# A plan of expert blocks worked out one stage earlier, and fewer clearings of semaphores between stages

## Chip, cores and metric

One core of one Trainium2 chip. The metric is the device time of one execution in microseconds. Its median over three runs of the kernel before is 2325.03 us.

## What is computed

Two layers, each an attention part and a mixture-of-experts part, over 16 sequences of 512 tokens and 128 features. After each part the result is added to its input and normalised:

```python
x = layernorm(x + L0_attn(x))   # cumulative sums over the sequence, 16 heads
x = layernorm(x + L0_ffn(x))    # top-1 of 8 experts, relu MLP 128-256-128
x = layernorm(x + L1_attn(x))   # softmax attention, 16 heads, position bias
x = layernorm(x + L1_ffn(x))    # shared swiglu + top-1 of 8 swiglu experts
```

In the expert parts every token goes through the one expert that its router picks: `expert = argmax(logits)`, `out[t] = MLP_expert[t](x[t])` (times a probability in the first layer, on an input times a score in the second).

## The kernel before

The program runs five stages one after the other (`program`, lines 2171 to 2219): `attention_one`, `experts` with tag b, `attention_two`, `experts` with tag d, and `finish`. Each stage has its own block of per-engine programs (`with nc.Block()`, lines 284, 938, 1249, 2042), at whose end every engine drains and all meet at a barrier. Behind it the helper `stage` (lines 2186 to 2191) lets GpSimd clear the stage's semaphores (line 2189) and then holds a second barrier of all engines (line 2190), five times in all, the last time behind `finish`.

Both attention stages loop over the 16 sequences and route their tokens at the end of each: VectorE keeps a running count of each expert's tokens (`keep.run`), works out the slot of every token, and GpSimd scatters the rows by indirect DMA to `xs_d` or `zs_d` (lines 647 and 1367, four DMAs for each sequence), so that every expert has a region of its own. At the end of the stage GpSimd waits for its scatters.

`experts` works in 24 blocks of 512 rows. Which expert and which rows a block has follows from the counts, so VectorE first works out a **plan** (lines 977 to 1015): some 20 small operations on 128x8, 128x24 and 128x192 elements, with a wait for its own semaphore between most of them. They make the two integer tables `expert` and `row` (24 entries each), and `offs`. GpSimd sets a tile of ones for it (line 967). SyncE waits for `plan_ready` 1 (the table `expert`) and 2 (the table `row`), and then, for each block, reads one value of each table into registers (line 906) and starts the load of the block's rows `x` (line 953) and of the expert's weights `w` (line 954), up to four blocks ahead of the work; the output goes out at line 959. TensorE turns the rows (line 1093), multiplies by the first weights (line 1085) and the second (line 1106), ScalarE and VectorE evict. After the plan VectorE also computes `keep.rows` (lines 1021 to 1034), which the next stage's gathers read. In the first expert stage GpSimd meanwhile splits and spreads a line of position biases for `attention_two` (lines 910 to 936), with loads and stores on its own queue.

What sets the order at a boundary, in SyncE's program of `experts`:

```python
sp.wait_ge(sem("plan_ready"), 1)
...
e = which(sp, expert, s.b, E - 1)
if isinstance(s.b, int) and s.b == 0:
    sp.wait_ge(sem("plan_ready"), 2)
r = which(sp, row, s.b, SPARE)
...
sp.dma_start(x[s.par][:], rows_of(src, r)).then_inc(sem(f"x_in{s.par}"), 16)
```

Of the kernel before, what the change touches and what calls it, by code (L numbers as in the profile page):

```python
# [14 lines left out]
I32 = mybir.dt.int32  # L15
# [4 lines left out]
P = 128  # L20
# [29 lines left out]
class Step:  # L50
# [3 lines left out]
    def __init__(self, b, half, par, mod=2):  # L54
        self.b, self.half, self.par, self.mod = b, half, par, mod
# [112 lines left out]
    own.wait()  # L168


def clear_rows(eng, name, b, io, done):

    regions = io[name][0:SPARE, :].rearrange("(e r) w -> e r w", e=E)
    eng.dma_start(regions[:, bass.ds(GROUP * b, GROUP), :].rearrange("e (p t) w -> p e (t w)", t=T),
                  io["zeros"].unsqueeze(1).to_broadcast([P, E, T * W])).then_inc(done, 16)
# [6 lines left out]
def attention_one(nc, g, keep):  # L182
# [9 lines left out]
    with ExitStack() as ctx:  # L192
        def sb(name, shape, dt=F32):
            return ctx.enter_context(nc.sbuf_tensor(name, shape, dt))
# [10 lines left out]
        total_ps = misc[:, T * E:2 * T * E].rearrange("p (t e) -> p t e", t=T)  # L205
        sel_ps = misc[:, 2 * T * E:3 * T * E].rearrange("p (t e) -> p t e", t=T)

        wk = sb("wk", [P, 3 * H])
        wv = sb("wv", [P, HA])
        wo = sb("wo", [P, HA // P, W])  # L210
# [73 lines left out]
        with nc.Block() as block:  # L284
# [396 lines left out]
            def _(dve):  # L681
# [158 lines left out]
                own.wait()  # L840
                own.did(v.tensor_copy(keep.run[:], runs[:, 0, :]))
                own.wait()


def experts(nc, g, keep, tag, src, dst, weights, gated):
# [14 lines left out]
    def sem(name):  # L860
        return g.sem(f"{tag}_{name}")

    with ExitStack() as ctx:
        def sb(name, shape, dt=F32):
            return ctx.enter_context(nc.sbuf_tensor(f"{tag}_{name}", shape, dt))
# [4 lines left out]
        count = sb("count", [P, E])  # L870
        blocks = sb("blocks", [P, E])
        ones8 = sb("ones8", [P, E])
        ends = sb("ends", [P, E])
        offs = sb("offs", [P, E])
        first = sb("first", [P, E])
        past = sb("past", [P, BLOCKS, E])
        ef = sb("ef", [P, BLOCKS])
        isf = sb("isf", [P, BLOCKS, E])
        rowf = sb("rowf", [P, BLOCKS])
        spare = sb("spare", [P, BLOCKS])  # L880
        row = sb("row", [P, BLOCKS], I32)
        expert = sb("expert", [P, BLOCKS], I32)
# [22 lines left out]
        def which(eng, table, n, top):  # L905
            return eng.value_load(table[0:1, bass.ds(n, 1)], min_val=0, max_val=top)
# [31 lines left out]
        with nc.Block() as block:  # L938

            @block.sync  # L940
            def _(sp):
                sp.wait_ge(sem("plan_ready"), 1)

                def step(s, on):
                    if on[0]:
                        e = which(sp, expert, s.b, E - 1)
                        if isinstance(s.b, int) and s.b == 0:
                            sp.wait_ge(sem("plan_ready"), 2)
                        r = which(sp, row, s.b, SPARE)
# [12 lines left out]
                for k in range(4):  # L962
                    sp.wait_ge(sem(f"y_out{k}"), 16 * BLOCKS // 4)

            @block.gpsimd
            def _(pool):
                nc.gpsimd.memset(ones8[:], 1.0).then_inc(sem("ones8_ready"), 1)
                if not gated:
                    split_line(pool)
                    spread_line(pool)  # L970

            @block.vector
            def _(dve):
                v = nc.vector
                own = Own(dve, sem("own"), sem("dve_passed"))
                dve.wait_ge(sem("ones8_ready"), 1)
                own.did(v.tensor_scalar(offs[:], keep.iota[:], float(REGION), None, ALU.mult))
                own.did(v.tensor_scalar(first[:], keep.iota[:], float(REGION), None, ALU.mult))
                own.wait()

                own.did(v.tensor_tensor(count[:], keep.run[:], offs[:], ALU.subtract))
                own.wait()
                own.did(v.tensor_scalar(blocks[:], count[:], GROUP - 1.0, 1.0 / GROUP, ALU.add, ALU.mult))
                own.wait()
                own.did(v.tensor_scalar(blocks[:], blocks[:], 0.5 / GROUP - 0.5, None, ALU.add))
                own.wait()
                own.did(v.tensor_scalar(blocks[:], blocks[:], ROUND, ROUND, ALU.add, ALU.subtract))
                own.wait()
                own.did(v.tensor_tensor_scan(ends[:], ones8[:], blocks[:], 0.0, ALU.mult, ALU.add))
                own.wait()  # L990

                many = [P, BLOCKS, E]
                own.did(v.tensor_tensor(past[:], keep.turn[:].unsqueeze(2).to_broadcast(many),
                                        ends[:].unsqueeze(1).to_broadcast(many), ALU.is_ge))
                own.wait()
                own.did(v.tensor_reduce(ef[:], past[:], AX, ALU.add))
                own.did(v.tensor_tensor(count[:], ends[:], blocks[:], ALU.subtract))
                own.wait()
                v.tensor_scalar(expert[:], ef[:], E - 1.0, None, ALU.min).then_inc(sem("plan_ready"), 1)

                own.did(v.tensor_tensor(isf[:], keep.iota[:].unsqueeze(1).to_broadcast(many),
                                        ef[:].unsqueeze(2).to_broadcast(many), ALU.is_equal))
                own.did(v.scalar_tensor_tensor(offs[:], count[:], -float(GROUP), offs[:], ALU.mult, ALU.add))
                own.did(v.tensor_scalar(spare[:], ef[:], E - 0.5, None, ALU.is_ge))
                own.did(v.tensor_scalar(rowf[:], keep.turn[:], float(GROUP), None, ALU.mult))
                own.wait()
                own.did(v.tensor_scalar(spare[:], spare[:], float(SPARE), None, ALU.mult))
                own.did(v.tensor_tensor(past[:], offs[:].unsqueeze(1).to_broadcast(many),
                                        rowf[:].unsqueeze(2).to_broadcast(many), ALU.add))
                own.wait()  # L1010
                own.did(v.tensor_tensor(past[:], past[:], isf[:], ALU.mult))
                own.wait()
                own.did(v.tensor_reduce(rowf[:], past[:], AX, ALU.add))
                own.wait()
                v.tensor_tensor(row[:], rowf[:], spare[:], ALU.add).then_inc(sem("plan_ready"), 1)
                dve.wait_ge(sem("plan_ready"), 2)


                pairs = [P, NB * T, E]
                slots = keep.slots[:].unsqueeze(2).to_broadcast(pairs)  # L1020
# [9 lines left out]
                own.did(v.tensor_tensor(its[:], its[:], offs[:].unsqueeze(1).to_broadcast(pairs), ALU.mult))  # L1030
# [85 lines left out]
def attention_two(nc, g, keep):  # L1116
# [20 lines left out]
    with ExitStack() as ctx:  # L1137
        def sb(name, shape, dt=F32):
            return ctx.enter_context(nc.sbuf_tensor(f"c_{name}", shape, dt))
# [10 lines left out]

        wq, wk, wv, wout = (sb(n, [P, W]) for n in ("wq", "wkk", "wvv", "wout"))
        gw = sb("gw", [P, E])
        x1 = sb("x1", [P, T, W])
        yb = sb("yb", [P, T, W])
        rows = sb("rows", [P, T], U32)
# [93 lines left out]
        with nc.Block() as block:  # L1249
# [467 lines left out]
            def _(dve):  # L1717
# [271 lines left out]
                route_last(s)  # L1989
                route_runs(s)  # L1990
                route_slots(s)


def finish(nc, g, keep):
# [180 lines left out]
def program(nc, io, stages=5):  # L2175
    g, keep = Bag(), Bag()
    g.io = io
    with ExitStack() as ctx:
# [4 lines left out]
                sems[name] = nc.alloc_semaphore(name=name)  # L2183
            return sems[name]

        def stage(run, *args):

            run(nc, g, keep, *args)
            nc.clear_and_free_semaphores(list(sems.values()))
            nc.all_engine_barrier()  # L2190
            sems.clear()

        def sb(name, shape, dt=F32):
            return ctx.enter_context(nc.sbuf_tensor(name, shape, dt))
# [9 lines left out]
        keep.prob = sb("prob", [P, NB * T])  # L2204
        keep.slots = sb("slots", [P, NB * T])
        keep.rows = sb("rows", [P, NB * T], U32)
        keep.bias = sb("bias", [P, H, DELTA, P])
        stage(attention_one)
        keep.line = sb("spread_line", [P, H, DELTA, UPAD], BF16)
        if stages >= 2:  # L2210
            stage(experts, "b", "xs_d", "ys_d", "wb", False)
        if stages >= 3:
            stage(attention_two)
        if stages >= 4:
            stage(experts, "d", "zs_d", "us_d", "wd", True)
        if stages >= 5:
            stage(finish)


_SCRATCH = {"line_d": ([H, DELTA * UPAD], F32), "bias_d": ([H, P, DELTA, P], F32), "x1_d": ([NB, P, T, W], F32), "xs_d": ([ROWS, W], F32),  # L2220
# [79 lines left out]
```

## Time and profile before

| | us |
|---|---|
| median of three runs (2323.05 to 2331.76) | 2325.03 |
| the profiled execution, whole | 2327.71 |
| its span, first to last instruction | 2325.9 |
| TensorE busy | 1985.4 (85%) |
| VectorE busy | 1502.4 (65%) |
| ScalarE busy | 1078.8 (46%) |
| GpSimd busy | 807.6 (35%) |
| mean granted TensorE clock | 0.939 of full speed |

The stages lie one behind the other in the span: the first ends at 628, the second at 765, the third at 2037 and the fourth at 2192 us. Register, branch, semaphore and DMA-issuing instructions do not count as busy; a view of one line shows them with their durations, with a q behind the engine's name for its sequencer.

### The profile page before, as it was taken

How to read it: one execution, taken by the hardware profiler on the slowest of the kernel's cores; microseconds unless marked ns; L12 is line 12 of the kernel's file. 1: busy time of each engine (PE TensorE's matmuls, PEld its weight loads, DVE VectorE, ACT ScalarE, POOL GpSimd, SP SyncE). 2: the span in 40 equal slices, each digit the busy share in tenths (PEclk: the TensorE clock that was granted, in tenths of full speed). 3: DMA queues.
4: the chain of work that ended last, by engine and by line, in shares of the span. 5: the costliest groups of instructions: out<-in, count | busy, mean ns of one | idle time of the engine just before them, and what ended most of it. 6: DMA issues, size and time to landing. Idle time of an engine off the chain costs nothing. (4 is left out here: it accounts for less than half of the span.)

```text
span 2325.9 us, 49229 instructions
## 1 busy us (share of the span) xinstructions
PE 1985.4 (85%) x15436; PEld 1034.3 (44%) x15436; DVE 1502.4 (65%) x4596; ACT 1078.8 (46%) x2723; POOL 807.6 (35%) x827
## 2 busy tenths in 40 slices
PE   8488787877388499999999999999999999679886
PEld 6255555655356133334333333334333433356554
DVE  6268878888511577777767767677677767233276
ACT  3355565565133045555555555455555555322221
POOL 4458888888400302221222122212221120100176
PEclk9689999999699699999999999999999999889998
DMA  3453232222187222322132213322232211144332
GB/s 111 153 181 109 105 104 100 75 104 98 45 229 221 91 72 80 100 84 95 61 97 92 87 61 96 95 85 86 72 103 82 96 59 64 56 140 158 115 104 86
DMA packets 127737, 235.72 MB, mean 101 GB/s; under 512 B 17622, under 2 KB 45286, under 8 KB 126966
## 3 DMA queue, kind: packets, MB, share of 16 engines
q1 hardware_dynamic: 118440, 208.51, 27.2%
q0 software_dynamic: 9072, 24.41, 3.7%
q8 instruction: 117, 1.92, 0.3%
q14 instruction: 108, 0.88, 0.1%
HBM read 185.88 MB, written 121.95 MB: 132 GB/s over the span
## 5 line engine op out<-in xcount | busy, mean ns | idle before, releaser
L1622 ACT ACTIVATE c_pT<-c_u 128x512 f32<-128x512 f32 x1024 | 574.6, 596 | 552.1 <-PE c_u L1429 552.1
L1777 DVE CUSTOM_DVE_ANT_0 c_sums<-c_s,bias 128x512 f32<-128x512 f32 x1024 | 665.1, 687 | 254.2 <-PE c_s L1411 229.5
L1411 PE MATMUL c_s<-c_kst,c_qst 126*128 126x512 bf16 x1024 | 319.0, 389 | 16.9 <-issue 11.5
L1429 PE MATMUL c_u<-spread_line,c_pick 128*32 128x512 bf16 x4096 | 317.2, 387 | 0.0
L1443 PE MATMUL c_o<-c_pT,c_vst 128*32 128x256 f32 x4096 | 310.9, 381 | 0.6 <-ACT c_pT L1622 0.5
L1421 PE MATMUL c_u<-c_qst,c_kst 128*128 128x512 bf16 x1024 | 307.7, 381 | 0.2 <-ACT c_pT L1622 0.2
L523 ACT ACTIVATE v<-a_bank,gain 128x64 f32<-128x64 f32 x768 | 166.4, 345 | 54.9 <-DVE vp L737 54.9
L1367 POOL DMA_INDIRECT zs_d<-c_xs,c_slot x64 | 63.4, 991 | 328.0 <-DMA zs_d<-in_zeros 190.6
L1443 PEld LDWEIGHTS c_o<-c_pT,c_vst 128*32 128x32 f32 x4096 | 123.1, 110 | 107.4 <-ACT c_pT L1622 4.0
L389 PE MATMUL a_bank<-wv,xT 128*128 128x512 f32 x256 | 154.1, 690 | 19.1 <-ACT v L523 14.2
L590 POOL TENSOR_TENSOR q<-q,vp 128x1024 f32<-128x1024 f32 x48 | 125.0, 2604 | 105.6 <-DVE vp L737 104.8
L1429 PEld LDWEIGHTS c_u<-spread_line,c_pick 128*32 128x32 bf16 x4096 | 61.8, 94 | 217.7 <-issue 217.7
L1421 PEld LDWEIGHTS c_u<-c_qst,c_kst 128*128 128x128 bf16 x1024 | 100.2, 98 | 121.1 <-issue 5.8
L1411 PEld LDWEIGHTS c_s<-c_kst,c_qst 126*128 126x128 bf16 x1024 | 82.7, 100 | 158.9 <-DVE c_tops L1777 101.9
L601 POOL TENSOR_TENSOR s<-q,v 128x1024 f32<-128x1024 f32 x48 | 143.3, 2985 | 0.2
L531 ACT COPY oT<-a_bank 128x512 f32<-128x512 f32 x128 | 69.4, 587 | 150.0 <-PE a_bank L410 149.9
L737 DVE TENSOR_TENSOR vp<-a_bank,ez 128x512 f32<-128x512 f32 x96 | 64.8, 687 | 106.8 <-PE a_bank L389 105.0
L418 PEld LDWEIGHTS a_bank<-wo,oT 128*128 128x128 f32 x1024 | 126.7, 199 | 14.4 <-issue 14.4
L418 PE MATMUL a_bank<-wo,oT 128*128 128x128 f32 x1024 | 129.2, 282 | 0.0
L753 DVE TENSOR_TENSOR o<-o,r 128x1024 f32<-128x1024 f32 x64 | 124.5, 1965 | 0.0
L410 PE MATMUL a_bank<-ident,o 128*128 128x128 f32 x512 | 79.2, 305 | 52.6 <-DVE o L753 51.8
L1356 POOL TENSOR_TENSOR c_rstd<-c_ve,minus_half 128x4 f32<-128x4 f32 x16 | 16.7, 1046 | 298.4 <-DVE c_ve L1746 298.4
(266 smaller groups left out, 2901.3 us busy)
## 6 DMA issues: line engine op xcount, KB each, us to landing
xs_d<-in_zeros SPq DMA_DIRECT2D x16, 2048.0 KB
zs_d<-in_zeros SPq DMA_DIRECT2D x16, 2048.0 KB, 10.0
c_kst<-parts_d SPq DMA_DIRECT2D x192, 96.0 KB
c_qst<-parts_d SPq DMA_DIRECT2D x192, 96.0 KB
parts_d<-c_parts SPq DMA_DIRECT2D x32, 384.0 KB, 3.1
d_w<-in_wd SPq DMA_DIRECT2D x24, 384.0 KB, 3.2
b_w<-in_wb SPq DMA_DIRECT2D x24, 321.0 KB, 4.6
bias_d<-line_d SPq DMA_DIRECT2D x16, 448.0 KB
```

Of the source, the lines that this page charges most:

```text
L389: nc.tensor.matmul(v_ps[h][:], xT[s.par][:, t, :], wv[:, 512 * h:512 * h + 512], start=True, stop=True).then_inc(sem("v_ready"), 1)
L418: mm = nc.tensor.matmul(y_ps[:, t * W:(t + 1) * W], oT[t % 2][:, k, :], wo[:, k, :], start=(k == 0), stop=(k == HA // P - 1))
L523: ins = nc.scalar.activation(dst[:, h * A:(h + 1) * A], v_ps[half][:, k * A:(k + 1) * A], ACT.Copy, scale=gain[s.par][:, t, h:h + 1])
L590: nc.gpsimd.tensor_tensor(q[:, t, :], q[:, t - 1, :], vp[t % 2][:], ALU.add).then_inc(sem("q_ready"), 1)
L601: nc.gpsimd.tensor_tensor(s1[s.par][:, t, :], q[:, t - 1, :], v2[t % 2][:], ALU.add).then_inc(sem("s1_ready"), 1)
L753: v.tensor_tensor(heads(o[t % 2][:]), heads(o[t % 2][:]), r[s.par][:, t, :].unsqueeze(2).to_broadcast([P, H, A]), ALU.mult).then_inc(sem(" ...
L1411: nc.tensor.matmul(s_ps[bank_of(n)][:], qst[0:ROWS_MAX, h, t * P:(t + 1) * P], kst[0:ROWS_MAX, h, :], start=True, stop=True).then_inc(sem( ...
L1421: nc.tensor.matmul(u_ps[bank_of(n)][:], kst[:, h, c * P:(c + 1) * P], qst[:, h, :], start=True, stop=False, skip_group_check=True)
L1429: mm = nc.tensor.matmul(u_ps[bank_of(n)][ARRAY * k:ARRAY * (k + 1), :].rearrange("k (t q) -> k t q", t=T), pick[:], line[:, G * j + i, T - ...
L1443: mm = nc.tensor.matmul(o_ps[ARRAY * i:ARRAY * (i + 1), half * 2 * P:(half + 1) * 2 * P], vst[s.par][:, c, f:f + ARRAY], pT[r % 2][:, i, h ...
L1622: nc.scalar.activation(pT[n // G % 2][:, n % G, :], u_ps[bank_of(n)][:], ACT.Exp).then_inc(sem("exp_done"), 1)
L1777: v.tensor_tensor_reduce(sums[n % 2][:], s_ps[bank_of(n)][:], bias, 1.0, -3.0e38, ALU.add, ALU.max, top_s[j % 2][:, k:k + 1]).then_inc(sem ...
```

## The change

A new function `plan` holds the operations of the plan, with its own memset of the ones on VectorE. It is called at the end of VectorE's program in `attention_one` (behind the copy to `keep.run`) and in `attention_two` (behind the slots of the last sequence). The tables `expert`, `row` and `offs` are kept across stages; the scratch tiles are allocated in the attention stages. `experts` loses the operations, the memset on GpSimd and both waits of SyncE. The clearing of semaphores with its barrier is now called once between the stages, ahead of `attention_two`, and once at the end; behind `attention_one`, `attention_two` and the second `experts` only the block's own barrier is left.

```diff
+def plan(v, own, keep, p):
+    many = [P, BLOCKS, E]
+    own.did(v.memset(p.ones8[:], 1.0))
+    own.did(v.tensor_scalar(keep.offs[:], keep.iota[:], float(REGION), None, ALU.mult))
+    own.wait()
+    own.did(v.tensor_tensor(p.count[:], keep.run[:], keep.offs[:], ALU.subtract))
...
+    own.did(v.tensor_scalar(keep.expert[:], p.ef[:], E - 1.0, None, ALU.min))
...
+    own.did(v.tensor_tensor(keep.row[:], p.rowf[:], p.spare[:], ALU.add))
+    own.wait()
@@ attention_one, end of VectorE's program
                 own.did(v.tensor_copy(keep.run[:], runs[:, 0, :]))
                 own.wait()
+                plan(v, own, keep, planner)
@@ experts, SyncE
-                sp.wait_ge(sem("plan_ready"), 1)
-
                 def step(s, on):
                     if on[0]:
-                        e = which(sp, expert, s.b, E - 1)
-                        if isinstance(s.b, int) and s.b == 0:
-                            sp.wait_ge(sem("plan_ready"), 2)
-                        r = which(sp, row, s.b, SPARE)
+                        e = which(sp, keep.expert, s.b, E - 1)
+                        r = which(sp, keep.row, s.b, SPARE)
@@ experts, GpSimd
-                nc.gpsimd.memset(ones8[:], 1.0).then_inc(sem("ones8_ready"), 1)
@@ experts, VectorE
-                dve.wait_ge(sem("ones8_ready"), 1)
-                own.did(v.tensor_scalar(offs[:], keep.iota[:], float(REGION), None, ALU.mult))
                 own.did(v.tensor_scalar(first[:], keep.iota[:], float(REGION), None, ALU.mult))
                 own.wait()
-                own.did(v.tensor_tensor(count[:], keep.run[:], offs[:], ALU.subtract))
...
-                v.tensor_tensor(row[:], rowf[:], spare[:], ALU.add).then_inc(sem("plan_ready"), 1)
-                dve.wait_ge(sem("plan_ready"), 2)
@@ attention_two, end of VectorE's program
                 route_slots(s)
+                own.wait()
+                plan(v, own, keep, planner)
@@ program
-        def stage(run, *args):
-            run(nc, g, keep, *args)
+        def clear():
             nc.clear_and_free_semaphores(list(sems.values()))
             nc.all_engine_barrier()
             sems.clear()
+        def stage(run, *args):
+            run(nc, g, keep, *args)
...
         if stages >= 3:
+            clear()
             stage(attention_two)
...
         if stages >= 5:
             stage(finish)
+        clear()
```

## Rows read from the trace of the kernel before

**Rows 1.** Waits, 600 to 640 us: engine, line, waited for; us, times, longest.
```profile
PE b_bank L1093 <- DMA b_x<-xs_d: 24.3, 1, 24.3
```

**Rows 2.** Timeline, 614 to 640 us: start, us, engine, line, operation, [idle before].
```profile
615.05 0.17 DVE L841 COPY run<-runs 128x8 f32<-128x8 f32 x1
616.00 1.07 POOL L647 DMA_INDIRECT xs_d<-x,slot  x1 [3.67 <-DVE slot L800]
...
619.91 0.96 POOL L647 DMA_INDIRECT xs_d<-x,slot  x1 [0.30 <-issue]
...
628.93 0.17 DVE L977 TENSOR_SCALAR b_offs<-iota 128x8 f32<-128x8 f32 x1 [13.71 <-POOL b_ones L967]
...
633.50 0.53 DVE L1015 TENSOR_TENSOR b_row<-b_rowf,b_spare 128x24 int32<-128x24 f32 x1
...
634.82 0.36 SPq L953 DMA_DIRECT2D b_x<-xs_d  x1
...
637.72 1.11 PE L1093 MATMUL b_bank<-ident,b_x 128*128 128x128 f32 x4 [24.28 <-DMA b_x<-xs_d]
```

**Rows 3.** Line 284, first block: ns min/median/max, first and last start.
```profile
L284 POOLq DRAIN  x1: 5304/5304/5304, 622.4 to 622.4; - x1
L284 SPq EVENT_SEMAPHORE  x1: 17/17/17, 627.8 to 627.8; - x1
```

**Rows 4.** Timeline, 2028 to 2047 us.
```profile
2028.40 0.16 DVE L1878 CAST c_slot<-c_slotf 128x4 uint32<-128x4 f32 x1
...
2033.28 0.96 POOL L1367 DMA_INDIRECT zs_d<-c_xs,c_slot  x1 [0.30 <-issue]
...
2038.32 0.17 DVE L977 TENSOR_SCALAR d_offs<-iota 128x8 f32<-128x8 f32 x1 [9.75 <-POOL d_ones L967]
...
2039.62 0.36 DVE L993 TENSOR_TENSOR d_past<-turn,d_ends 128x192 f32<-128x192 f32 x1
...
2042.46 0.18 DVE L1015 TENSOR_TENSOR d_row<-d_rowf,d_spare 128x24 int32<-128x24 f32 x1
...
2043.42 0.37 SPq L953 DMA_DIRECT2D d_x<-zs_d  x1
```

**Rows 5.** Line 1249, block of attention_two.
```profile
L1249 POOLq DRAIN  x1: 1367/1367/1367, 2035.7 to 2035.7; - x1
L1249 SPq EVENT_SEMAPHORE  x1: 17/17/17, 2037.2 to 2037.2; - x1
```

**Rows 6.** Line 906, table reads of SyncE, 2037 to 2044 us.
```profile
L906 SPq TENSOR_LOAD <-d_expert x1: 480/480/480, 2040.7 to 2040.7; - x1
L906 SPq TENSOR_LOAD <-d_row x1: 274/274/274, 2042.7 to 2042.7; - x1
```

**Rows 7.** Line 2189, the clearing of semaphores, whole execution.
```profile
L2189 POOLq EVENT_SEMAPHORE_RANGE_CLEAR  x5: 156/182/418, 628.1 to 2325.0; - x5
```

**Rows 8.** Line 2189, 620 to 630 us.
```profile
L2189 POOLq EVENT_SEMAPHORE_RANGE_CLEAR  x1: 397/397/397, 628.1 to 628.1; - x1
```

**Rows 9.** Line 938, block of the second experts stage, 2190 to 2193 us.
```profile
L938 SPq EVENT_SEMAPHORE  x1: 17/17/17, 2191.6 to 2191.6; - x1
```

**Rows 10.** Line 2190, the barrier behind the clearing, 2190 to 2193 us.
```profile
L2190 SPq EVENT_SEMAPHORE  x1: 17/17/17, 2192.1 to 2192.1; - x1
```

**Rows 11.** Line 647, scatter of attention_one, all 64.
```profile
L647 POOL DMA_INDIRECT xs_d<-x,slot x64: 957/962/2815, 193.5 to 619.9; - x64
```

**Rows 12.** Timeline, 2223.6 to 2226 us, in finish.
```profile
2224.11 0.68 DVE L2161 TENSOR_TENSOR e_part<-e_x,e_routed 128x512 f32<-128x512 f32 x1
...
2224.20 1.42 POOL L2075 DMA_INDIRECT e_routed<-us_d,e_rows  x1 [0.30 <-issue]
```

**Rows 13.** Windows: stretch, length; busy us (count) per engine; clock, DMA, GB/s.
```profile
650.00:700.00 50.00, 41.27 (x227) 29.09 (x226) 6.23 (x9) 17.88 (x28) 4.43 (x9) 0.93 0.89 241
767.00:804.00 37.00, 13.77 (x27) 5.63 (x27) 19.92 (x44) 4.33 (x10) 14.54 (x18) 0.50 0.30 91
825.00:900.00 75.00, 73.83 (x732) 27.57 (x729) 52.32 (x168) 43.42 (x88) 8.99 (x11) 1.00 0.24 76
```

More of the change, by code:

```diff
@@ L168, in slots_of, with __init__ @@
     own.wait()
+class Planner:
+    def __init__(self, sb):
+        self.count, self.blocks, self.ones8, self.ends = (sb(f"plan_{n}", [P, E]) for n in ("count", "blocks", "ones8", "ends"))
+        self.past, self.isf = (sb(f"plan_{n}", [P, BLOCKS, E]) for n in ("past", "isf"))
+        self.ef, self.rowf, self.spare = (sb(f"plan_{n}", [P, BLOCKS]) for n in ("ef", "rowf", "spare"))
+def plan(v, own, keep, p):
[5 more added lines that the diff above has]
+    own.wait()
+    own.did(v.tensor_scalar(p.blocks[:], p.count[:], GROUP - 1.0, 1.0 / GROUP, ALU.add, ALU.mult))
+    own.wait()
+    own.did(v.tensor_scalar(p.blocks[:], p.blocks[:], 0.5 / GROUP - 0.5, None, ALU.add))
+    own.wait()
+    own.did(v.tensor_scalar(p.blocks[:], p.blocks[:], ROUND, ROUND, ALU.add, ALU.subtract))
+    own.wait()
+    own.did(v.tensor_tensor_scan(p.ends[:], p.ones8[:], p.blocks[:], 0.0, ALU.mult, ALU.add))
+    own.wait()
+    own.did(v.tensor_tensor(p.past[:], keep.turn[:].unsqueeze(2).to_broadcast(many),
+                            p.ends[:].unsqueeze(1).to_broadcast(many), ALU.is_ge))
+    own.wait()
+    own.did(v.tensor_reduce(p.ef[:], p.past[:], AX, ALU.add))
+    own.did(v.tensor_tensor(p.count[:], p.ends[:], p.blocks[:], ALU.subtract))
+    own.wait()
+    own.did(v.tensor_scalar(keep.expert[:], p.ef[:], E - 1.0, None, ALU.min))
+    own.did(v.tensor_tensor(p.isf[:], keep.iota[:].unsqueeze(1).to_broadcast(many),
+                            p.ef[:].unsqueeze(2).to_broadcast(many), ALU.is_equal))
+    own.did(v.scalar_tensor_tensor(keep.offs[:], p.count[:], -float(GROUP), keep.offs[:], ALU.mult, ALU.add))
+    own.did(v.tensor_scalar(p.spare[:], p.ef[:], E - 0.5, None, ALU.is_ge))
+    own.did(v.tensor_scalar(p.rowf[:], keep.turn[:], float(GROUP), None, ALU.mult))
+    own.wait()
+    own.did(v.tensor_scalar(p.spare[:], p.spare[:], float(SPARE), None, ALU.mult))
+    own.did(v.tensor_tensor(p.past[:], keep.offs[:].unsqueeze(1).to_broadcast(many),
+                            p.rowf[:].unsqueeze(2).to_broadcast(many), ALU.add))
+    own.wait()
+    own.did(v.tensor_tensor(p.past[:], p.past[:], p.isf[:], ALU.mult))
+    own.wait()
+    own.did(v.tensor_reduce(p.rowf[:], p.past[:], AX, ALU.add))
+    own.wait()
+    own.did(v.tensor_tensor(keep.row[:], p.rowf[:], p.spare[:], ALU.add))
+    own.wait()
@@ L206, in attention_one @@
         sel_ps = misc[:, 2 * T * E:3 * T * E].rearrange("p (t e) -> p t e", t=T)
+        planner = Planner(sb)
         wk = sb("wk", [P, 3 * H])
@@ L869, in experts @@
         y_ps = [b[:].rearrange("p (t w) -> p t w", t=T) for b in bank[6:8]]
[L870 to L874, printed above, removed]
-        first = sb("first", [P, E])
[L876 to L882, printed above, removed]
+        first = sb("first", [P, E])
         chosen = sb("chosen", [P, NB * T])
@@ L975, in _ @@
                 own = Own(dve, sem("own"), sem("dve_passed"))
-                dve.wait_ge(sem("ones8_ready"), 1)
-                own.did(v.tensor_scalar(offs[:], keep.iota[:], float(REGION), None, ALU.mult))
                 own.did(v.tensor_scalar(first[:], keep.iota[:], float(REGION), None, ALU.mult))
                 own.wait()
-                own.did(v.tensor_tensor(count[:], keep.run[:], offs[:], ALU.subtract))
-                own.wait()
-                own.did(v.tensor_scalar(blocks[:], count[:], GROUP - 1.0, 1.0 / GROUP, ALU.add, ALU.mult))
@@ L984, in _ @@
[L984 to L1014, printed above, removed]
-                v.tensor_tensor(row[:], rowf[:], spare[:], ALU.add).then_inc(sem("plan_ready"), 1)
-                dve.wait_ge(sem("plan_ready"), 2)
                 pairs = [P, NB * T, E]
@@ L1029, in _ @@
                 own.wait()
-                own.did(v.tensor_tensor(its[:], its[:], offs[:].unsqueeze(1).to_broadcast(pairs), ALU.mult))
+                own.did(v.tensor_tensor(its[:], its[:], keep.offs[:].unsqueeze(1).to_broadcast(pairs), ALU.mult))
                 own.wait()
@@ L1152, in attention_two @@
         gw = sb("gw", [P, E])
+        planner = Planner(sb)
         x1 = sb("x1", [P, T, W])
@@ L1991, in _ @@
                 route_slots(s)
+                own.wait()
+                plan(v, own, keep, planner)
 def finish(nc, g, keep):
@@ L2206, in program @@
         keep.rows = sb("rows", [P, NB * T], U32)
+        keep.expert = sb("expert", [P, BLOCKS], I32)
+        keep.row = sb("row", [P, BLOCKS], I32)
+        keep.offs = sb("offs", [P, E])
         keep.bias = sb("bias", [P, H, DELTA, P])
```

## The prediction

> **What bounds the kernel now.** I start with the times: the span is 2325.9 us, the profiled execution took 2327.71 with what lies around it, 2.7 above the median of 2325.03. I work out a saving against that execution and take it off both. The change touches only the boundaries between stages, so the next view is the waits around the first of them: TensorE idles 24.3 us there, and what ends the wait is the landing of the first block's rows [rows 1]. The reader should ask what that load waited for. The timeline answers [rows 2]: GpSimd issues the last scatters of attention_one from 616.0 to 620.9, VectorE, free since 615.2, does nothing until 628.93, then works on the plan until 634.03, and only then does SyncE issue the load, at 634.82; TensorE starts 2.9 us behind it. What holds the barrier until 627.8 is GpSimd's drain, 5.30 us long, at the end of its block [rows 3]. The chain at the boundary is thus: scatters, drain, block barrier, clearing, second barrier, plan, table reads, load. The third boundary has the same chain [rows 4]: VectorE free at 2028.56, last scatter issued at 2034.24, drain of 1.37 us and barrier at 2037.2 [rows 5], plan from 2038.32 to 2042.64, load at 2043.42.
>
> **The plan leaves the chain (both experts stages).** In the changed kernel VectorE runs it from 615.2 and from 2028.6, beside the scatters. It takes 5.1 us in the first place, where GpSimd's work on the bias line ran beside it, and 4.3 us in the second [rows 2, 4]. Counted with 5.1 and a small memset more (0.17, as VectorE's smallest rows), it ends at about 620.4 and 2033.8, before the barriers at 627.8 and 2037.2 [rows 3, 5]: 7.4 and 3.4 us of cover. If that cover were gone, each us of the plan would delay the barrier by one. I cost it at nothing on VectorE's side. SyncE then goes on from the block barrier. It still has to read two tables: the first read took 0.48 us, the second 0.27, and from the start of the second to the load lie 0.72 us [rows 4, 6], so 0.45 us of register work for each table and 0.48 + 0.45 + 0.72 = 1.65 us in all; I take 1.7 for the barrier's own instruction too. First load of stage b: 627.8 + 1.7 = 629.5 instead of 634.82, **5.3 us** earlier. Stage d: 2037.2 + 1.7 = 2038.9 instead of 2043.42, **4.5 us** earlier. These two differences contain the clearing and second barrier that go at those places.
>
> Does a stage that starts earlier end earlier by as much? In stage b the DMA engines are busy 0.89 of the stretch from 650 to 700 with TensorE at 41.3 of 50 us [rows 13]; both are work that follows the first load and has no fixed hour, so I shift the whole stage. GpSimd's load of the bias line stands right behind the barrier in its program (line 914), so it moves with the barrier by less than 1 us while the blocks' loads move by 5.3, and comes to lie right beside the first x load. I cost the overlap at nothing and keep up to 1 us of it for the range. VectorE's next work, `keep.rows`, also starts at the barrier and not behind the plan, so nothing on its queue gets later; GpSimd's queue loses its memset and gains nothing.
>
> **The clearing.** Behind the second experts stage the block barrier is at 2191.6 and the one behind the clearing at 2192.1 [rows 9, 10]: **0.5 us** go. The clearing itself is not constant: 0.156 to 0.418 us [rows 7], with 0.397 behind attention_one [rows 8], which has by far more semaphores in its code than the experts stages. The instruction takes longer for more semaphores, so the two clearings that stay grow: ahead of attention_two by the 0.40 of attention_one, at the end by the largest and the smallest, 0.42 + 0.16. **Back: 1.0 us.** The lower bound is nothing (one instruction whatever the range), the upper one 1.0 again if a split range needs more instructions with their drains.
>
> **What the plan does to GpSimd.** This is the cost that the trace before doesn't show directly: VectorE is now busy beside the last four scatters of each attention stage, and the barrier hangs on those. An undisturbed scatter DMA takes 0.957 us, the longest 2.815 [rows 11]; in the last stage one takes 1.42 us when a VectorE operation with both inputs in SBUF starts just ahead of it [rows 12], 0.46 longer. The Trainium skill ("SBUF — State Buffer", "Who interferes with whom") says that such a tensor_tensor shares an interface with GpSimd's reads, but infers that descriptor generation isn't stalled by it, only by two-port operations such as tensor_scalar; by it the cost would be that of the tensor_scalars, well under 1 us. The trace disagrees with the inference in the 1.42 us row. By rows: nothing is the lower bound; the upper one is all eight two-input operations of the plan, four counted with 0.18 and four with 0.36 [rows 4], 2.2 us for each boundary, 4.4 in all. I take one delay of the size of that row for each boundary, 0.46, since the plan's operations are shorter than that one: **1.0 us** for both.
>
> **The sum.** 5.3 + 4.5 + 0.5 - 1.0 - 1.0 = 8.3 us. The profiled execution would take 2319.4 us, the median 2325.03 - 8.3 = **2316.7 us**, 0.36% less. A measurement of this kernel tells about 0.5%, 11.6 us, from no change, so the likeliest outcome lies within it.
>
> **Rivals.**
>
> *A drain changes its length.* GpSimd's drain took 5.30 us behind attention_one and 1.37 behind attention_two after the same four scatters [rows 3, 5], and I can't derive either from the trace. With VectorE at work beside the scatters the lengths may change. If the long one falls to the short one, 3.9 us more go: 2312.8 us, faster by 0.53%. Chance 0.12. If the short one grows to the long one, or the scatters are held up by the full 4.4 us, 3 to 4 us less: about 2320 us. Chance 0.15. For both speaks only that the two lengths exist; against, that the scatters' own issue is the same.
>
> *The first shift is swallowed.* The DMA engines at 0.89 [rows 13] and the bias line's traffic could make the first experts stage end at nearly the same time, as its early loads only queue. Then only 4.5 + 0.5 - 2.0 us are left: 2322 us. Against: no transfer in the stage waits for a clock. Chance 0.05. That the change doesn't do what it says (SyncE still held by something after the barrier) would look the same or worse; the code has no other wait ahead of the first loads, and I give it nothing of its own.
>
> *Slower: the TensorE clock at the start of attention_two.* From 767 to 804 us the granted clock is 0.50, the lower level of 1.2 GHz, while TensorE is busy for 13.8 of 37 us; from 825 on it is 1.00, 2.4 GHz, with TensorE busy for 73.8 of 75 us [rows 13]. The stage now begins some 4 us earlier and with other phases of its loads. If the low level came back for as long a stretch, 37 us, in the dense part, half of it, 18.5 us, would be lost: 2316.7 + 18.5 = 2335 us. The point from which it decides: more than 17 us of additional low clock in the dense part undoes the saving, 40 us make it slower by over 0.5%. For it speaks that the clock does fall after sparse stretches at every boundary; against, that the work and its order inside the stage are unchanged. Chance 0.05, of which 0.03 reaches past 0.5%.
>
> **How the numbers follow.** The forecast's chance is 0.63; its own spread is 2313 to 2320 from the bounds above (4.4 or nothing for the scatters, up to 2 for the clearings, some us of the clock, which rises and falls in steps at every boundary). The range is 2310 to 2323: it takes in both drain rivals and the swallowed shift, and leaves out the clock rival and a corner on either side. Faster by over 0.5% is below 2313.4: the drain rival's 0.12 and 0.14 of the forecast's lower edge, 0.26. Slower by over 0.5%: 0.03. Within 0.5%: 0.71.
>
> **What would show it.** In the changed profile the block barrier of the first stage should stand within 1 us of 627.8, and SyncE's first load of x 1.7 us behind it, without a plan on VectorE in between; VectorE's plan should stand beside the four scatters, and those should be at 0.96 to 1.4 us each. The length of stage b and of stage d from first x load to block barrier should be within 1 us of before. The clearing ahead of attention_two should read about 0.6 us, the one at the end about 0.75. The prediction is wrong if the drains behind the attention stages are other than 5.3 and 1.4 us, if scatters wait for VectorE by more than 1 us a boundary, or if attention_two's length from its first load to its last scatter changes by more than 3 us.

## The result and the profile after

The changed kernel took 2316.68 us (median of ten runs, 2312.69 to 2323.81) against 2326.41 us for the kernel before (ten runs, 2321.38 to 2331.76): ratio 0.9964, 95% interval 0.9950 to 0.9979. That is 9.7 us less where 8.3 were forecast, a difference from no change that ten runs of each can just tell, and within the 0.5% that the text called indistinguishable.

The waits around the first boundary, from 600 to 640 us of the changed kernel (line numbers have moved; L1088 is what L1093 was):

```profile
PE b_bank L1088 <- DMA b_x<-xs_d: 19.8, 2, 18.8
POOL b_whole L954 <- POOLq L335: 7.6, 1, 7.6
```

TensorE's wait is 18.8 us instead of 24.3 [rows 1]. The timeline of the same stretch shows why:

```profile
615.31 0.16 DVE L184 TENSOR_SCALAR offs<-iota 128x8 f32<-128x8 f32 x1
...
616.03 1.07 POOL L698 DMA_INDIRECT xs_d<-x,slot  x1 [3.67 <-DVE slot L851]
...
617.40 0.96 POOL L698 DMA_INDIRECT xs_d<-x,slot  x1 [0.30 <-issue]
...
617.96 0.39 DVE L207 TENSOR_SCALAR plan_rowf<-turn 128x24 f32<-128x24 f32 x1
...
618.67 0.98 POOL L698 DMA_INDIRECT xs_d<-x,slot  x1 [0.30 <-issue]
...
619.63 0.18 DVE L217 TENSOR_TENSOR row<-plan_rowf,plan_spare 128x24 int32<-128x24 f32 x1
...
619.95 0.96 POOL L698 DMA_INDIRECT xs_d<-x,slot  x1 [0.30 <-issue]
...
629.56 0.36 SPq L989 DMA_DIRECT2D b_x<-xs_d  x1
```

The plan, 628.93 to 634.03 before [rows 2], now runs from 615.31 to 619.81 beside the four scatters, which start and end within 0.1 us of where they did. The first x load is issued at 629.56; 629.5 was forecast. The end of the first block, view of line 335:

```profile
L335 POOLq DRAIN  x1: 5304/5304/5304, 622.4 to 622.4; - x1
L335 SPq EVENT_SEMAPHORE  x1: 17/17/17, 627.9 to 627.9; - x1
```

The end of attention_two's block, line 1245:

```profile
L1245 POOLq DRAIN  x1: 1362/1362/1362, 2026.8 to 2026.8; - x1
L1245 SPq EVENT_SEMAPHORE  x1: 17/17/17, 2028.4 to 2028.4; - x1
```

SyncE's table reads behind the first barrier, line 946 from 627 to 630 us:

```profile
L946 SPq TENSOR_LOAD <-expert x1: 490/490/490, 628.0 to 628.0; - x1
L946 SPq TENSOR_LOAD <-row x1: 282/282/282, 628.8 to 628.8; - x1
```

The clearings, line 2186, whole execution:

```profile
L2186 POOLq EVENT_SEMAPHORE_RANGE_CLEAR  x2: 527/602/677, 756.2 to 2313.0; - x2
```

Both drains kept their lengths [rows 3, 5]; the table reads take 0.49 and 0.28 us, where 0.48 and 0.27 were read before [rows 6]; the two clearings that are left take 0.53 and 0.68 us, longer than any before [rows 7]. The third boundary, timeline from 2018 us:

```profile
2019.54 0.16 DVE L184 TENSOR_SCALAR offs<-iota 128x8 f32<-128x8 f32 x1
...
2023.59 0.18 DVE L217 TENSOR_TENSOR row<-c_plan_rowf,c_plan_spare 128x24 int32<-128x24 f32 x1
...
2030.02 0.37 SPq L989 DMA_DIRECT2D d_x<-zs_d  x1
```

One of the eight scatters beside the plan is longer than before, the second at this boundary, 1.08 us where it took 0.96. It starts 0.10 us into a plan operation with two inputs:

```profile
2021.71 0.35 DVE L203 TENSOR_TENSOR c_plan_isf<-iota,c_plan_ef 128x192 f32<-128x192 f32 x1
2021.81 1.08 POOL L1363 DMA_INDIRECT zs_d<-c_xs,c_slot  x1 [0.31 <-issue]
```

The span fell from 2325.9 to 2314.0 us, by 11.9. I cut both traces at the same events, SyncE's barrier instructions and first x loads; all in us:

| stretch | before | changed | less |
|---|---|---|---|
| to the block barrier of attention_one | 627.85 | 627.89 | 0.0 |
| barrier to first x load, stage b | 6.97 | 1.67 | 5.3 |
| stage b, first x load to block barrier | 130.18 | 126.39 | 3.8 |
| clearing and second barrier ahead of attention_two | 0.58 | 1.04 | -0.5 |
| attention_two | 1271.63 | 1271.38 | 0.3 |
| barrier to first x load, stage d | 6.21 | 1.65 | 4.6 |
| stage d | 148.14 | 148.10 | 0.0 |
| clearing ahead of finish | 0.55 | 0 | 0.5 |
| finish | 132.67 | 134.56 | -1.9 |
| last clearing and end | 1.11 | 1.30 | -0.2 |

The change's own places are the five boundary rows: 5.3 + 4.6 + 0.5 - 0.5 - 0.2 = 9.7 us. The 0.1 us that the longer scatter costs lies inside attention_two. The 3.8 of stage b and the 1.9 of finish are not places that the change touches, and the experiments had to say whether they belong to it.

### The profile page after: what moved, and what is told of

It is laid out like the page before. It is cut to its first block and busy times, and to the rows that moved or that the text cites. A ratio compares the mean times of both kernels' runs of the same rounds, so it can differ in the third digit from the quotient of the medians.

```text
span 2314.0 us, 49191 instructions
## 1 busy us (share of the span) xinstructions
PE 1987.7 (86%) x15436; PEld 1032.6 (45%) x15436; DVE 1502.0 (65%) x4598; ACT 1077.6 (47%) x2723; POOL 807.1 (35%) x825
```

## The experiments

**The parts alone, the change again, and a first look at the drain.** All four ran together on a chip on which the kernel before took 2374.85 us (33 runs), so they compare with one another and not with the runs above. `plan_moved_alone` clears behind every stage again:

```diff
         def stage(run, *args):
             run(nc, g, keep, *args)
+            clear()
...
         if stages >= 3:
-            clear()
             stage(attention_two)
...
-        clear()
```

> The plan is moved as in the change; semaphores are still cleared, with the second barrier, behind every stage. Theory (the gain is the plan's and its table reads' leaving the chain): the block barrier of the first stage stays at 627.9 us and the first x load comes 1.7 us behind the second barrier, at 630.4; stage d's first load 1.7 us behind its barrier too. Against before some 4.4 + 3.7 = 8.1 us less, against the full change some 1 us more: about 2318 us. Rival (the clearings carry it): within 2 us of before, about 2325 us.

Measured: 2370.46 us, ratio 0.9970 (0.9948 to 0.9992), so 4.4 us less in the median where 8 was expected, with an interval of 2 to 12 us. Its trace has the mechanism: 1.66 us from the second barrier (649.63) to the first x load (651.29), 1.64 us in stage d. By the trace the rival of the clearings falls; the total alone, with an interval that begins at 2 us, would not have settled it.

`clear_moved_alone` is the kernel before with the `clear()` of the change:

> The plan stays in the experts stages; semaphores are cleared once ahead of attention_two and once at the end. Theory: 0.9 + 0.9 + 0.5 us of clearing and barrier go, 0.4 + 0.5 us come back in the two longer clearings: 1.4 us less than before, about 2325 us, which a measurement can't tell from no change. Rival (a shorter first experts stage, 126.4 us from first load to barrier in the changed kernel against 130.2 before, comes with the clearings): 4 us or more less.

Measured: 2374.09 us, ratio 0.9988 (0.9969 to 1.0007). No difference that can be told, as expected; from block barrier to first load it has 6.07 us in stage b, 0.9 less than before. But its stage b takes 127.72 us, not 130.

`changed_again` is the changed kernel without an edit:

> The changed kernel once more, for a second trace and as the standard of this job. If the 3.8 us by which the first experts stage was shorter in its trace (126.4 against 130.2 us from first load to block barrier) belong to the change, they are there again (within 1 us); if they are chance of an execution, the stage lies anywhere between 126 and 131 us. The same for finish, 1.9 us longer than before. Total about 2317 us.

Measured: 2369.44 us, ratio 0.9973 (0.9954 to 0.9991). Stage b: 127.96 us. `changed_third` and `changed_fourth`, again the changed kernel without an edit, beside the later runs, were expected to take:

> The changed kernel, as the standard of this job and a third trace of its stages. The first experts stage has taken 126.4 and 128.0 us from first load to block barrier with it, 126.5 and 131.8 in two variants that start the same way, 130.2 and 127.7 with the plan in the stage: chance, between 126 and 132 again, and no part of the change's gain.

> The changed kernel as the standard of this job, 8 to 10 us less than before.

They took 2317.95 us (ratio 0.9955, 0.9939 to 0.9971) and 2323.33 us (0.9956, 0.9933 to 0.9978), and stage b in them 127.67 and 124.62 us. In fourteen traces, those of the runs below included, stage b lies between 124.6 and 131.8 us: with the plan inside at 130.2, 127.7 and 131.7, with the plan moved at 124.6 to 131.8. The 3.8 us of the first pair of traces are at least in part chance. The means, 129.9 us of three traces and 127.8 of eleven, would leave 2 us to the plan's place; with three traces of one kind and a spread of 7 us that stays open.

`early_drain` asks why GpSimd's drain takes 5.30 us at the end of attention_one and 1.37 at the end of attention_two, which the prediction could not derive:

```diff
                 def route_scatter(s):
+                    if isinstance(s.b, int) and s.b == NB - 1:
+                        nc.gpsimd.drain()
@@ finish, GpSimd
                         b = s.back(2)
+                        if isinstance(b.b, int) and b.b == NB - 1:
+                            nc.gpsimd.drain()
```

> The changed kernel with one more drain on GpSimd ahead of the last sequence's scatters in attention_one and ahead of the last rstd in finish, where GpSimd has 2.9 and 4.4 us without work. Theory A (the 5.3 us drain is a cost that the first drain of a stage pays once, whenever it is called): the extra drain takes about 5.3 us, the one at the end of the block 1.4, and the first block barrier comes at about 626.4 instead of 627.9 us, the last one about 1 us earlier; 2.5 us less than the changed kernel. Theory B (the cost follows from the work just ahead of the drain, or comes with every drain): the extra drain is an addition, the last one still takes 5.3 us, the barrier comes at 628 to 630.5 us; 0 to 3 us more than the changed kernel.

The added drain, line 695:

```profile
L695 POOLq DRAIN  x1: 5820/5820/5820, 631.8 to 631.8; - x1
```

The one at the end of attention_one's block, line 335:

```profile
L335 POOLq DRAIN  x1: 380/380/380, 645.0 to 645.0; - x1
```

The one at the end of finish, line 2042:

```profile
L2042 POOLq DRAIN  x1: 1106/1106/1106, 2369.6 to 2369.6; - x1
```

The added one starts beside GpSimd's last 0.8 us of work, so 5.0 us are its own, and the last one is left with 0.38. In finish the drain before covered an operation of 1.0 us and lasted 6.34; now it ends with the operation, at 1.11, and the added one ends 5.30 us behind the work it covers. Theory A holds in this: the cost isn't tied to the end of the block. The move isn't free: the last scatters now wait for the added drain and start 3.2 us behind their slots instead of 1.0, so that the barrier comes 10.3 us behind the last slots instead of 12.9, 2.6 us earlier. 2366.48 us, ratio 0.9962 (0.9939 to 0.9985), 3 us below the changed kernel of the same job, inside the noise. And the numbers fit one count: 64 indirect DMAs since the drain before, 5.30 us; 60 of them, 5.0; the last 4, 0.38; 18 DMAs of GpSimd in stage b, 1.52. That is 83 to 95 ns for each.

**Drains in the gaps.** `drains` puts one ahead of every sequence's scatters, so that few DMAs are left at the end:

```diff
                 def route_scatter(s):
+                    nc.gpsimd.drain()
@@ attention_two, scatter(s), and finish, ahead of the last rstd
+                    if isinstance(s.b, int) and s.b == NB - 1:
+                        nc.gpsimd.drain()
```

> The changed kernel with further drains on GpSimd: one ahead of every sequence's scatters in attention_one, one ahead of the last sequence's scatters in attention_two, one ahead of the last rstd in finish. Theory (a drain costs about 83 ns for each software DMA issued since the drain before: 64 give 5.30, 18 give 1.52, 60 gave 5.0, 4 gave 0.38): the drains inside attention_one take about 0.35 us each in gaps, the one at its block's end 0.4 instead of 5.30, and the first barrier comes 4.9 us earlier; attention_two's end 1.0 and finish's 0.8 us earlier. 6.7 us less than the changed kernel. Rival (a drain costs 5 us once in a stage, however many DMAs): the first drain of attention_one takes some 5 us inside the loop, the others little; the same end. Rival (the drains hold up GpSimd's work in the loop): attention_one's loop gets longer by more than the 4.9 us.

The drain at the end of attention_one, line 335:

```profile
L335 POOLq DRAIN  x1: 375/375/375, 616.6 to 616.6; - x1
```

And at the end of attention_two, line 1246:

```profile
L1246 POOLq DRAIN  x1: 375/375/375, 2020.9 to 2020.9; - x1
```

2307.91 us against 2327.3 before, ratio 0.9925 (0.9903 to 0.9948), and against 2317.95 of the changed kernel in the same job. The drains inside the loop read 1.5 to 4.2 us each because they start while GpSimd's earlier work still runs, so their lengths alone don't judge the rival of a single 5 us drain. Their ends do. The last one, line 694, and the work beside it:

```profile
L694 POOLq DRAIN  x1: 1487/1487/1487, 605.4 to 605.4; - x1
```

```profile
605.32 1.17 POOL L690 TENSOR_SCALAR oh<-iota,idxf 128x8 f32<-128x8 f32 x4 [0.24 <-POOL idxf L685]
```

It ends at 606.89, 0.40 us behind that work. So do all fifteen that have four DMAs ahead of them, 0.40 to 0.41 us behind; the first drain, with none ahead, ends 0.07 behind. No drain of the loop costs 5 us, and the rival falls. What the three edits give can be read without the noise of the totals: from the last slots to the barrier 7.98 us instead of 12.89 in attention_one and 7.95 instead of 8.92 in attention_two, from the last gather to the barrier of finish 11.16 instead of 11.95. That is 4.9 + 1.0 + 0.8 = 6.7 us, the sum expected. The totals stand 10 us apart; what makes up the other 3 isn't shown. The loop of attention_one, from its first scatter to the first of the last sequence, took 420.5 us against 424.3 in the changed kernel's trace, but 434.8 against 432.4 in the pair of the next runs: no hold-up is shown, and no gain. Twice more:

> The changed kernel with the further drains, once more, beside the changed kernel itself. The drain terms give 4.9 us at the end of attention_one, 1.0 at the end of attention_two and 0.8 at the end of finish: 6.7 us less than the changed kernel. The medians of the first job stood 10 us apart with 6 and 8 runs; if the drains shorten attention_one's loop too, the 10 us are there again, if not, 7.

> The kernel before with the same further drains and nothing of the change. If the drain's length is a cost of its own, in the chain of both kernels, this is 6.7 us less than before, and the change's gain and the drains' add up. If the plan beside the scatters had anything to do with the drain, they wouldn't: nothing or more than 10 us.

`drains_again`: 2314.88 us, ratio 0.9922 (0.9896 to 0.9948), 8.5 us below the changed kernel of its job. `drains_on_before`, the same three edits on the kernel before: 2326.58 against 2331.34, ratio 0.9976 (0.9960 to 0.9992), 4.8 us less, with an interval of 2 to 9 us around the 6.7 expected. Its final drains of the attention stages read 0.375 us as well, and its first barrier comes 7.94 us behind the last slots instead of 12.87. The drain was a cost of its own in both kernels, and taking it away adds to the change.

**How much cover the plan has.** `plan_four_times`:

```diff
-                plan(v, own, keep, planner)
+                for _ in range(4):
+                    plan(v, own, keep, planner)
```

> The changed kernel with the plan worked out four times over at both places (same result). One plan took 4.5 us beside the scatters, so VectorE ends 18 us behind its start instead of 4.5. Theory (the plan is free as long as it ends ahead of GpSimd's drain, and costs one for one behind it): it ends 5.6 us behind the drain's end in attention_one and 8.5 behind it in attention_two, and the block barriers come later by just that: 14 us more than the changed kernel, with scatters and drain as they were. Rival (the plan's operations hold up the scatters, as the 1.42 us row had it): scatters of 1.1 us and more.

Line 335, the end of attention_one; drain and barrier:

```profile
L335 POOLq DRAIN  x1: 5304/5304/5304, 616.0 to 616.0; - x1
L335 SPq EVENT_SEMAPHORE  x1: 17/17/17, 626.8 to 626.8; - x1
```

The drain ends at 621.35 and the barrier comes 5.4 us later; in attention_two 9.0 us later (2032.23 to 2041.21). 5.6 and 8.5 were expected. Seven of the eight scatters took 0.96 to 1.07 us, one 1.08, as with one plan. The total, a single run, is 2330.13 us, 12 more than the changed kernel's median, where 14 were expected. So the plan is free up to the drain's end and costs one for one behind it; with one plan 7.9 us of the cover are unused in attention_one (plan's end at 619.8, drain's at 627.7) and 4.4 in attention_two. (With the drains moved, attention_one's cover shrinks to about 3 us, still enough.)

**The shared SBUF interface.** `probe_ports` adds VectorE work beside the last scatters; the results don't depend on it:

```diff
@@ attention_one, ahead of plan
+                for _ in range(7):
+                    own.did(v.tensor_tensor(probe[:, 0], probe[:, 0], probe[:, 1], ALU.mult))
+                    own.wait()
@@ attention_two, ahead of plan
+                for _ in range(14):
+                    own.did(v.tensor_scalar(sums[0][:], sums[1][:], 2.0, None, ALU.mult))
+                    own.wait()
```

> The changed kernel with VectorE work added between the last slots and the plan: in attention_one seven tensor_tensor operations on 128x448 with both inputs in SBUF, in attention_two fourteen tensor_scalar operations on 128x512 from SBUF to SBUF, each row of them beside the last four scatters. By the prediction's reading of the 1.42 us row, each scatter beside a two-input operation takes up to 0.5 us longer: four scatters of 1.2 to 1.5 us in attention_one, and about 0.97 in attention_two. By the Trainium skill's inference it is the other way: 0.96 in attention_one, and longer ones, up to the length of the operations beside them, in attention_two.

The total, a single run, is 2323.12 us; the work added in attention_two outlasts the drain, so the total says nothing of the scatters. Timeline of the first place:

```profile
613.09 4.58 DVE L898 TENSOR_TENSOR probe<-probe 128x448 f32<-128x448 f32 x7
613.83 1.48 POOL L699 DMA_INDIRECT xs_d<-x,slot  x1 [3.67 <-DVE slot L854]
615.62 0.96 POOL L699 DMA_INDIRECT xs_d<-x,slot  x1 [0.30 <-issue]
616.89 0.96 POOL L699 DMA_INDIRECT xs_d<-x,slot  x1 [0.30 <-issue]
618.15 0.96 POOL L699 DMA_INDIRECT xs_d<-x,slot  x1 [0.30 <-issue]
```

Timeline of the second, where the scatters stand beside tensor_scalars of 0.43 us:

```profile
2025.11 1.04 POOL L1369 DMA_INDIRECT zs_d<-c_xs,c_slot  x1 [11.30 <-DVE c_slot L1880]
2026.45 0.96 POOL L1369 DMA_INDIRECT zs_d<-c_xs,c_slot  x1 [0.30 <-issue]
2027.71 1.21 POOL L1369 DMA_INDIRECT zs_d<-c_xs,c_slot  x1 [0.31 <-issue]
2029.23 1.22 POOL L1369 DMA_INDIRECT zs_d<-c_xs,c_slot  x1 [0.30 <-issue]
```

Neither expectation came out whole. Under two-input operations one scatter of four is longer (1.48 us where the first takes 1.07), under tensor_scalar two are (1.21, started with 0.38 us of one to run; the first, with 0.46, took the usual 1.04). The long one of the first place started 0.09 us into an operation of 0.63, so 0.54 of it were still to run, and it was 0.42 longer; the next two started with 0.07 and 0.12 us left and show nothing. It fits the row of the kernel before: the gather of 1.42 us started with 0.59 us of the operation to run and took 0.46 more [rows 12]. A scatter thus waits at its start for a two-input operation under way, and not for those that begin later.

The 64 gathers of finish in each of the fourteen traces say the same with more cases. 137 of them started with 0.58 to 0.59 us to run of the operation of line 2161 (2159 in the changed kernel; both inputs in SBUF), and all took 1.41 to 1.42 us; no other gather did. 20 started with 0.31 to 0.66 us to run of an operation that has one of its two inputs in PSUM, and took 0.94 to 0.96: what sets them apart from the first kind is where the second input lies. And two-input operations aren't alone: 90 gathers that started with 0.23 to 0.25 us of a tensor_scalar from SBUF to SBUF to run took 1.13 to 1.16 us (49 others, with 0.26 to 0.27 us left, took 1.03). The plan's own operations fit too: 0.25 us of one left made a scatter 0.12 longer, 0.15 left 0.02 longer, and in `early_drain` 0.29 left 0.16 longer.

**That collision in finish.** In the thirteen traces of kernels that keep this operation finish repeats a sequence every 6.8 or 7.4 us once it runs, with 7 to 12 gathers of 1.42 us an execution, 7 in the kernel before and 9 in the changed one. Two collisions more, at 0.5 to 0.6 us each, are some 1.1 of the 1.9 us of the first pair; of the rest, 0.4 us lie in the second sequence and 0.5 behind the last gather, and no run shows why. The two traces with the least, 7 and 8, are of kernels that have nothing of the change, but each part alone shows 12, so what sets their number stays open. Timeline of `changed_third`, from a period with a collision and from one without:

```profile
2243.14 0.68 DVE L2159 TENSOR_TENSOR e_part<-e_x,e_routed 128x512 f32<-128x512 f32 x1
...
2243.23 1.42 POOL L2073 DMA_INDIRECT e_routed<-us_d,e_rows  x1 [0.30 <-issue]
...
2250.52 0.95 POOL L2073 DMA_INDIRECT e_routed<-us_d,e_rows  x1 [0.30 <-issue]
...
2250.57 0.68 DVE L2159 TENSOR_TENSOR e_part<-e_x,e_routed 128x512 f32<-128x512 f32 x1
```

An operation that starts 0.09 us ahead of the gather costs it half a us; one that starts 0.05 us behind it costs nothing. `residual_in_psum`, on top of `drains`, takes the operation away and lets TensorE add the input of the residual. Its edit in finish, without the smaller number of semaphore steps of VectorE:

```diff
@@ TensorE
-                                mm = nc.tensor.matmul(y_ps[b.par % 2][:, t, :], h[b.par % 2][:, c, t, :], sd[:, c, :],
-                                                      start=(c == 0), stop=(c == CHUNKS - 1))
+                                nc.tensor.matmul(y_ps[b.par % 2][:, t, :], h[b.par % 2][:, c, t, :], sd[:, c, :],
+                                                 start=(c == 0), stop=False)
+                            mm = nc.tensor.matmul(y_ps[b.par % 2][:, t, :], keep.ident[:], x3[b.par][:, t, :],
+                                                  start=False, stop=True)
@@ VectorE
-                        dve.wait_ge(sem(f"x3_in{b.par}"), 16 * b.half + 16)
...
-                        own.did(v.tensor_tensor(part[:], x3[b.par][:], routed[b.par][:], ALU.add))
-                        own.wait()
+                        need(dve, sem("out_ready"), b.b)
                         dve.wait_ge(sem("y_ps"), b.b + 1)
-                        v.tensor_tensor(xr[:], y_ps[b.par % 2], part[:], ALU.add).then_inc(sem("y_read"), 1)
+                        v.tensor_tensor(xr[:], y_ps[b.par % 2], routed[b.par][:], ALU.add).then_inc(sem("y_read"), 1)
```

> The kernel with the further drains, and in finish the input of the residual added by TensorE in PSUM (four matmuls with the identity for each sequence) instead of by a VectorE operation with two SBUF inputs. In the traces so far finish repeats one sequence every 6.8 or 7.4 us, and every period of 7.4 has one gather DMA of 1.42 us that lies beside that VectorE operation: 7 to 12 of them an execution, and finish is 1 to 3 us longer where there are more. Theory (that collision sets the difference): no gather over 1.1 us is left, every period is 6.8 us or less, and finish takes some 129 us from barrier to barrier instead of 135.5, 6 us less than with the drains alone, 22 us less than before. Rival (the periods are set by something else, such as TensorE, which gets 0.5 us more work a sequence): periods stay at 7.4, finish at 135 us or more.

The gathers of finish, all 64:

```profile
L2076 POOL DMA_INDIRECT e_routed<-us_d,e_rows x64: 940/951/1153, 2180.3 to 2296.2; - x64
```

Line 2076 is the gather's. None is over 1.16 us, the periods are 6.8 to 7.0, and finish takes 129.46 us, 129 expected, against 134.87 and 135.50 in the two traces with the drains alone. The collision is what set the difference: the operation that went is also 0.68 us of VectorE's work in every sequence, but the periods without a collision are 6.8 us with it and without it, so that work did not set them. The total is 2324.15 us against 2340.75 before on that chip, ratio 0.9917 (0.9894 to 0.9941). Whether it is faster than `drains` (0.9922 and 0.9925) the ratios can't say: the two never ran in one job, and the intervals overlap by far. Both lie below the changed kernel's 0.9955 to 0.9973.

## Why the prediction was right

**The chain.** That the plan, the table reads and a barrier stood between GpSimd's drain and the first x load, and that nothing else did, is shown by the first loads 1.67 and 1.65 us behind the barriers (1.7 forecast): 5.3 and 4.6 us against 5.3 and 4.5.

**The shift of the stages.** Stage d took 148.14 and 148.10 us, attention_two 1271.63 and 1271.38: an earlier start is an earlier end. For stage b the single pair of traces would have told a better story than is true; fourteen traces have it anywhere within 7 us. The sign that stage b would keep its length within 1 us failed in the first pair of traces (3.8 us), and stage b does not keep it between executions of one kernel either (124.6 to 128.0 us in four of the changed one). The rival of the swallowed first shift falls, since stage b was not longer in any standard of the changed kernel than the 130.2 us of before.

**The clearings.** 0.5 us forecast for the one ahead of finish, 0.5 measured. Back: 1.0 forecast, 0.7 measured. The instruction grew by a little less than reckoned, from 0.18 to 0.53 (0.58 reckoned) and to 0.68 (0.76), but in the kernel before 0.34 us of idle time lay behind the last one, and behind the longer one they don't.

**The scatters.** This term was mis-sized: 1.0 us forecast, 0.1 measured. Seven of the eight scatters kept their lengths within 0.02 us and one took 1.08 us instead of 0.96; from the last slots to the barrier attention_one took 12.88 us against 12.87, attention_two 8.91 against 8.81, and every trace with one plan moved and the drains untouched has it so within 0.01. I had charged each boundary with one full collision of the 1.42 us row. The probe shows that a collision costs what is left of an operation at the scatter's start, and the plan's two-input operations last 0.36 us at most. (The upper bound counted eight of them; the scan of line 194 is a ninth.) VectorE pays instead: line 207 took 0.39 us, not 0.17, beside the scatters of attention_one, under the cover of the drain. The inference of the Trainium skill ("SBUF — State Buffer", "Who interferes with whom") came out no better: it would have excluded the long scatter of the probe, 1.48 us. What it says of tensor_scalar agrees with two of four scatters, at 1.21 us.

**The drains.** Both kept their lengths, so that rival fell on both sides. What I couldn't derive was not the change's doing but goes with a count of DMAs, and was worth another 6.7 us at the ends of three stages.

**The clock.** From barrier to barrier attention_two took 1271.63 and 1271.38 us, and the mean granted clock is 0.939 in both profiles. The slower rival did not come.

**The sum.** With the terms as measured it is 5.3 + 4.6 + 0.5 - 0.7 - 0.1 = 9.6 us: 1.3 more than forecast, nearly all of it from the scatters' term and the clearings'. That the medians differ by 9.7 is luck to the tenth. Their interval is 5 to 12 us, and the other three pairs of medians stand 5.4, 9.4 and 8.0 us apart.

## What to carry to other kernels

At a boundary between stages, look at what the last engine to arrive is doing and at every engine that idles meanwhile: work that depends on nothing of the last engine's is free there up to that engine's drain, as long as it doesn't hold up that engine's own work, and costs one for one behind it. Read the drain itself too; if GpSimd has issued many DMAs, a drain in an earlier gap may be worth nearly as much as the moved work (4.9 against 5.3 us at the first boundary here). The gap has to be long enough, or the drain holds up what follows it. And before a stage that got shorter or longer by a few us is credited to a change, look at the same stage in several traces of the same kernel.

## What was not expected of the hardware

In this kernel a GpSimd drain takes some 83 ns for each DMA that GpSimd has issued since the drain before: 5.30 us for 64, 1.52 for 18, 0.38 for 4. Attention_two doesn't fit: it issues 128, and its drain takes 1.36 us, what 16 would cost; with an added drain ahead of its last four scatters 0.375 are left, as elsewhere, and the added one, behind 124 of them, costs 1.07 us, what 12 would. Why the other 112 aren't counted stays open.

A gather or scatter DMA of GpSimd waits at its start for a VectorE operation with two inputs in SBUF that is under way: 0.42 us more with 0.54 us left of it, 0.46 with 0.59, 0.12 with 0.25, nothing with 0.12 or less, and nothing where one input is in PSUM (20 gathers with 0.31 to 0.66 us left). Some tensor_scalars from SBUF to SBUF do it too. Whether it comes to that is a matter of 0.1 us of phase: 7 to 12 such gathers an execution, at 0.5 to 0.6 us each, are up to 3 us of finish (an estimate from its periods of 6.8 and 7.4 us).
